# A deformable-convolution sampler regrouped by source rows, its TensorE part in a register-addressed loop

## What is computed

```
ys = base_y[None, None, :, None] + (ky * dil)[None, :, None, None] + dy
xs = base_x[None, None, None, :] + (kx * dil)[None, :, None, None] + dx
...
s = gather(img, y0b, x0b) * w00[None] + gather(img, y0b, x0b + 1) * w01[None] + gather(img, y0b + 1, x0b) * w10[None] + gather(img, y0b + 1, x0b + 1) * w11[None]
...
off1 = conv2d(x, w_off1, b_off1, stride=1, pad=1)
out = jax.nn.relu(bn_inf(deform_conv(x, off1, w_dc1, 1, 2, 2), g1, beta1, m1, v1))
off2 = conv2d(out, w_off2, b_off2, stride=1, pad=1)
out = bn_inf(deform_conv(out, off2, w_dc2, 1, 2, 2), g2, beta2, m2, v2)
out = out + x
return jax.nn.relu(out)
```

## Time and profile before

| | |
|---|---|
| three runs | 892.66, 894.47, 895.07 us; median 894.47 |
| profiled execution | 889.64 us, span 887.6 us |
| PE busy | 728.3 us (82%) |
| DVE, ACT, POOL busy | 484.3, 417.0, 161.4 us |
| mean granted TensorE clock | 0.86 |
| first sampler, from its first coordinates to the last ACT output | 40.1 to 257.4 us |
| second sampler, likewise | 286.1 to 507.0 us |
| attention and experts | 507 to 887.6 us |

### The profile page before, as it was taken

The page is one execution under the profiler, slowest core; times in us unless marked ns, Lnnn a source line. Parts: engine busy times, 40 slices in busy tenths (PEclk is TensorE's granted clock), DMA queues, the critical chain, the costliest instruction groups (busy, mean ns, idle before and its releaser), DMA issues.

```text
span 887.6 us, 40461 instructions
## 1 busy us (share of the span) xinstructions
PE 728.3 (82%) x18746; PEld 567.3 (64%) x18746; DVE 484.3 (55%) x840; ACT 417.0 (47%) x830; POOL 161.4 (18%) x190
## 2 busy tenths in 40 slices
PE   6787877788767887778788656999999999999546
PEld 2355555566633455555566545999999999998433
DVE  0565554455604645446455564666666666666654
ACT  1665455554315554546544143445445445545442
POOL 7000000000030000000000153343443443341300
PEclk8889878866769798887976578999999999999669
DMA  5400000000004000000000170000000000000002
GB/s 171 82 4 5 4 4 5 5 4 4 5 6 81 4 5 4 4 4 4 5 4 4 29 193 1 1 2 1 0 0 0 0 0 0 0 0 0 0 1 96
DMA packets 7835, 16.58 MB, mean 19 GB/s; under 512 B 1982, under 2 KB 5950, under 8 KB 7286
## 3 DMA queue, kind: packets, MB, share of 16 engines
q1 hardware_dynamic: 7678, 14.21, 6.3%
HBM read 10.34 MB, written 3.87 MB: 16 GB/s over the span
## 4 chain that ended last, share of the span: by engine, by line
PE 76%; issue 10%; DVE 6%; ACT 5%; POOL 1%; DMA 1%; SPq 0%; DVEq 0%
PE banks L227 20%; PE banks L145 14%; PE banks L696 7%; PE banks L680 7%; PE banks L726 6%; PE banks L458 4%; PE banks L737 4%; PE banks L716 3%; PE banks L691 2%; PE banks L180 2%; PE banks L166 2%; PE banks L707 2%; ACT hx L273 1%; DVE norm_stats L629 1%; ACT hy L278 1%
## 5 line engine op out<-in xcount | busy, mean ns | idle before, releaser
L227 PE MATMUL banks<-s,y 32*64 32x96 f32 (+9 forms) x10752 | 191.1, 268 | 66.0 <-issue 65.9
L318 DVE TENSOR_TENSOR s<-hy,hx 128x384 f32<-128x384 f32 (+3 forms) x336 | 144.4, 476 | 183.4 <-PE banks L227 181.8
L227 PEld LDWEIGHTS banks<-s,y 32*64 32x64 f32 x10752 | 160.2, 154 | 109.9 <-issue 100.2
L145 PE MATMUL banks<-w_dc,tiled 64*32 64x192 f32 x3584 | 130.2, 412 | 20.3 <-issue 13.7
L268 ACT COPY y<-banks 128x384 f32<-128x384 f32 x192 | 81.8, 484 | 114.0 <-PE banks L145 114.0
L145 PEld LDWEIGHTS banks<-w_dc,tiled 64*32 64x32 f32 x3584 | 74.3, 131 | 53.8 <-issue 26.6
L794 ACT COPY hy<-banks 128x512 f32<-128x512 f32 x64 | 37.6, 588 | 116.7 <-PE banks L726 116.7
L278 ACT ACTIVATE hy<-banks 128x512 f32<-128x512 f32 (+2 forms) x144 | 72.9, 583 | 38.4 <-PE banks L180 38.3
L898 POOL TENSOR_TENSOR y<-y,stats 128x1024 f32<-128x1024 f32 x33 | 62.8, 1902 | 142.2 <-DVE stats L839 142.2
L273 ACT ACTIVATE hx<-banks 128x384 f32<-128x384 f32 x144 | 61.4, 505 | 31.8 <-PE banks L166 23.9
L680 PE MATMUL banks<-src,s 128*128 (+1 forms) x560 | 75.0, 279 | 1.1 <-ACT src L617 1.1
(11 more groups left out here) (137 smaller groups left out, 876.9 us busy)
## 6 DMA issues: line engine op xcount, KB each, us to landing
src<-in_x_dram SPq DMA_DIRECT2D x4, 578.0 KB, 5.5
y<-in_w_dram SPq DMA_DIRECT2D x1, 2080.0 KB
off<-in_w_dram SPq DMA_DIRECT2D x2, 1024.0 KB
out_dram<-tokens SPq DMA_DIRECT2D x4, 512.0 KB, 2.6
offsets_dram<-tokens SPq DMA_DIRECT2D x32, 54.0 KB
off<-offsets_dram SPq DMA_DIRECT2D x16, 108.0 KB
w_dc<-in_w_dc_dram SPq DMA_DIRECT2D x2, 288.0 KB, 6.0
y<-in_w_attn_dram SPq DMA_DIRECT2D x1, 512.0 KB, 4.9
```

What stands on the lines that cost most here:

```text
L145: last = nc.tensor.matmul(m.ps[32 * j:32 * j + 32, FIRST_BANK + (count + g) % RING, (col % 2) * 192:(col % 2) * 192 + 192], m.tiled[rows, ...
L227: last = nc.tensor.matmul(out[:, r0:r0 + strip.n, first:first + width], m.y[32 * j:32 * j + 32, g, (s // 3) % 2 * Y_SLOTS + strip.slot, co ...
L318: nc.vector.tensor_tensor(dst, hy, hx[:, :, r0:r0 + strip.n, :], ALU.mult).then_inc(cv.s_ready, 1)
```

## The change

The sampler is regrouped. The outer loop now goes over the 8 source tile rows, the inner over the 9 taps: 72 steps per convolution, each with all 8 output rows of the window, inside the image or not.

- **PE** runs the 8 tile rows as a loop `with pe.Fori(0, TR) as i` with one body of nine taps; addresses in `off` and the values waited for come from registers.
- **Output.** A tile row adds into a 12-row band in PSUM (banks 0 to 3, 384 columns of each). After each tile row ACT copies the new rows to `tokens` in SBUF, DVE adds the band of the row before (L351), PE clears it.
- **x hats** are made for four new rows per step; the four others come from the block kept from the tile row before. So `s` is made by two products of 384 elements.
- **Slots.** An item (x, y or weighted) uses a pair of banks, two slots in turn; ACT takes a pair out with one instruction instead of two.
- **Weighted tiles** (`stage`, `yk`) are made for one tile row, three `ky` in six halves per row, placed behind the sampling of steps 0, 4, 5, 6, 7 and 8.
- **Coordinates** are built over all 128 partitions of `off` with a wider selection matrix (`near_sel`, 983 KB more to load), in six matmuls per step.
- **At the start** DVE clears `off` before the loads into it; the sampler waits for `moved[0]` and `moved[1]`; five weighted items instead of eight pairs come before it.
- The products and outputs of rows outside the image are not used.

```diff
+FIRST_COORDS = [("x", tap, -1) for tap in range(3)] + coords(0) + coords(1) + [("x", tap, -1) for tap in range(3, 6)]
+AHEAD = 2
+STEP_WEIGHTED = {0: (2, 1, 0), 4: (0, 0, 1), 5: (0, 1, 1), 6: (1, 0, 1), 7: (1, 1, 1), 8: (2, 0, 1)}
...
+def sampler_pe(nc, pe, m, cv):
+    old = 2 * cv.reach
+    for half in range(HALVES):
+        pe.wait_ge(cv.moved[half], MOVES)
...
+    with pe.Fori(0, TR) as i:
+        k = BEFORE_LOOP
+        for t in range(TAPS):
+            later, tap = divmod(t + AHEAD, TAPS)
+            pe.wait_ge(cv.emptied, i * PER_ROW + (k - 1))
+            columns_near(nc, m, cv, k, tap, new_rows(cv, tap) + TILE_ROWS * later, TILE_ROWS, i)
+            k += 1
+            pe.wait_ge(cv.emptied, i * PER_ROW + (k - 1))
+            rows_near(nc, m, cv, k, tap, first_row(cv, tap) + TILE_ROWS * later, i)
+            k += 1
+            if t == 0:
+                pe.wait_ge(cv.copied, i + COPIED_FROM)
+                pe.wait_ge(cv.added, i + (ADDED_FROM - 1))
+                pe.wait_ge(cv.cleared, 1)
+                for bank in range(PAIRS):
+                    nc.tensor.matmul(m.ps[:, bank, 0:OUT_ROWS * W], m.zeros[:, 0:P], m.zeros[:, 0:OUT_ROWS * W],
+                                     start=True, stop=True, skip_group_check=True)
+            if t in STEP_WEIGHTED:
+
+                pe.wait_ge(cv.emptied, i * PER_ROW + (k - 1))
...
+            pe.wait_ge(cv.s_ready, i * (2 * TAPS) + (2 * t + 2))
+            for col in range(TC):
...
+                                                s_rows(m, cv, t)[32 * j:32 * j + 32, :, g, at:at + width],
+                                                start=False, stop=True, skip_group_check=True)
+            last.then_inc(cv.sampled, 1)
+            if t in STEP_WEIGHTED:
+                weighted_near(nc, m, cv, k, *STEP_WEIGHTED[t][0:2])
+                k += 1
...
+def weighted_act(nc, act, m, cv, k, ky, part):
+    act.wait_ge(cv.filled, k + 1)
+    nc.scalar.copy(m.yk[:, ky, :, 2 * part:2 * part + 2, :].rearrange("p g a n -> p g (a n)"),
+                   slot_banks(m, k)[:, :, 0:384]).then_inc(cv.emptied, 1)
...
+    for tile_row in range(TR):
+        for t in range(TAPS):
+            if t == 2 and tile_row >= 2:
+                cv.rows_act(act, tile_row - 2)
+            for kind, *_ in step_items(tile_row, t):
+                if t == TAPS - 1 and kind == "w" and tile_row < TR - 1:
+                    act.wait_ge(cv.sampled, TAPS * (tile_row + 1))
...
+                    nc.scalar.copy(sum_rows(m, at, n), out_rows(m, first, n)).then_inc(cv.copied, 1)
+                item_act(nc, act, m, cv, k)
+                k += 1
...
+    for n in range(TR * TAPS):
+        if n + 1 < TR * TAPS:
+            hats(n + 1)
...
+        if n % TAPS == 0 and n // TAPS >= 2:
+            below = n // TAPS - 1
+            dve.wait_ge(cv.sampled, n)
+            dve.wait_ge(cv.copied, COPIED_FROM + below + 1)
...
+        weights(n)
```

More of the change, by code:

```diff
@@ L55, in near_strips @@
[L55 to L71, removed]
@@ L74, in near_columns @@
[L74 to L125, removed]
@@ new lines, in step_items @@
+def step_items(tile_row, tap):
+    items = coords(TAPS * tile_row + tap + AHEAD)
+    if tap in STEP_WEIGHTED:
+        ky, part, later = STEP_WEIGHTED[tap]
+        items.append(("w", ky, part, tile_row + later))
+    return items
+BEFORE_LOOP = len(FIRST_WEIGHTED) + len(FIRST_COORDS)
+PER_ROW = sum(len(step_items(0, tap)) for tap in range(TAPS))
+ITEMS = FIRST_WEIGHTED + FIRST_COORDS + [
+    item for tile_row in range(TR) for tap in range(TAPS) for item in step_items(tile_row, tap)]
+EMPTIED_AT = {item: k + 1 for k, item in enumerate(ITEMS)}
@@ new lines, with slot_banks, window, near_columns @@
+assert PER_ROW % 2 == 0
+def slot_banks(m, k):
+    return m.ps[:, FIRST_BANK + 2 * (k % 2):FIRST_BANK + 2 * (k % 2) + 2, :]
+def window(cv):
+    return TILE_ROWS + 2 * cv.reach, TILE_COLS + 2 * cv.reach, 2 - cv.reach
+def near_columns(cv, c, kx):
+    _, cols, ahead = window(cv)
+    at = TILE_COLS * c + ahead - 2 * kx
+    first = max(at, 0)
+    return first, min(at + cols, W) - first, first - at
+def weighted_near(nc, m, cv, k, ky, part):
+    for col in (2 * part, 2 * part + 1):
+        for j in range(4):
+            for g in range(2):
+                image = IMAGES[g][j]
+                rows = slice(C * (image % 2), C * (image % 2) + C)
+                last = nc.tensor.matmul(
+                    m.ps[32 * j:32 * j + 32, FIRST_BANK + 2 * (k % 2) + g, (col % 2) * 192:(col % 2) * 192 + 192],
+                    m.stage[rows, image // 2, col, :], cv.w_dc[rows, 3 * ky:3 * ky + 3, :],
+                    start=True, stop=True, skip_group_check=True)
+    last.then_inc(cv.filled, 1)
@@ new lines, in columns_all @@
+def columns_all(nc, pe, m, cv, count, h, tap, col):
+    pe.wait_ge(cv.all_emptied, count - RING + 2)
+    for g in range(2):
+        rows = group_rows(g, 1)
+        nc.tensor.matmul(m.ps[:, FIRST_BANK + (count + g) % RING, :],
+                         m.sel[rows, (TILE_COLS * col - 2 * (tap % 3) + 4) // 2, :],
+                         m.off[rows, tap, HALF_ROWS * W * h:HALF_ROWS * W * (h + 1)],
+                         start=True, stop=True, skip_group_check=True).then_inc(cv.all_filled, 1)
```

579 lines of the change are left out of this document (345 added, 234 removed).

## The result

The changed kernel takes 968.18 us (median of 4 runs, 967.68 to 971.83) against 894.77 us: a ratio of 1.0818 with a 95% interval of 1.076 to 1.0876, slower by 73 us. Forecast were 927 us and a range of 873 to 965. All times are medians of a kernel's runs on one chip beside new runs of the kernel before; two kernels, e1_pad2 and e7_pad50, have one run each in a slower state of the chip, and their other runs alone have medians of 923.5 and 923.9 us.

A forecast was written before the change was run, and what follows sets the result against it. PE was taken to be bound by its instruction supply, 128 matmuls per 3.73 us. Profiled 889.6 us, plus 33 for 16 tile rows of 28.0 us and their ends, plus 4.8 to the median, gave 927 us, range 873 to 965.

The forecast's parts named there:

- the loop stays: Likeliest case, both samplers: PE's loop isn't fetched anew, steps paced by the two-slot chain; +4 to +57 us, chance 0.48.
- rival 3: PE's loop body doesn't stay, one packet's 3.73 us per back edge: +42 us on top of +33, 948 to 969 us, chance 0.20.
- a two-slot chain: Sampler steps: PE in order with two slots, next sampling waits behind ACT's emptying of the weighted item; 25.7 us per row.
- Weighted step: Six of nine sampler steps: sampling, weighted products, ACT's copy, hand-overs and y coordinates in series, 3.06 us at clock 1.00.
- The other steps: Three sampler steps without weighted products: coordinates, ACT, hat and products, 4.0 us spread over two steps, 2.0 us each.
- The row boundary: End of a tile row: ACT's copy and DVE's sum before PE may clear, about 1.3 us left over, bounds 0.4 and 2.4.
- The clock: PE's mean granted clock in the samplers taken as 0.85, 70% of the time at 1.00, against 0.80 before.
- R = 28.0: Sampler time per tile row at the mixed clock, 28.0 us; with change = 16R − 415.1 it gives +33 us.
- Rival 2: Faster, the samplers' chain is short enough: R below 25.9 us, such as clock 1.00 throughout; 871 to 891 us, chance 0.26.
- Beginnings: Samplers wait for both halves of the offsets and so start later: +1.7 us in the first, +2.9 us in the second.
- Costed at nothing: Clearing of `off`, larger tables (+7 us if not hidden), stage copies, address instructions (+52 us if on the path), wider coordinate matmuls.
- The rule: Against the change: loop body of 6.7 packets, 31% more than any loop shown to stay, just fills or passes 8 blocks.

The follow-up runs named there:

- e1_pad2: Changed kernel with 30 tiny matmuls of zeros ahead of the second sampler's coordinates: 928.07 us, ratio 1.0307 to the kernel before.
- e7_pad50: Changed kernel with 50 tiny matmuls of zeros ahead of the second sampler's coordinates: 926.04 us, ratio 1.0242 to the kernel before.
- e9_again: Changed kernel once more, unaltered, on the same chip as the padded ones: 972.39 us, ratio 1.0857 to the kernel before.
- e11_pad30: Second run of the changed kernel with 30 tiny matmuls of zeros ahead of the second sampler's coordinates: 923.41 us, ratio 1.030 to the kernel before.
- e3_short: Changed kernel with only 6 tiny matmuls of zeros ahead of the second sampler's coordinates: 992.08 us, ratio 1.0999 to the kernel before.

## Why the prediction was wrong, point by point

**What bounds the kernel before: right.** One packet of 128 matmuls per 3.73 us. The written-out kernels draw 6 or 7 packets per row as computed.

**The step that failed: "the loop stays", taken for both convolutions from the body's length.** The prediction counted 6.7 packets for the body, saw that with the partly used blocks at both ends they just fill or pass 8 blocks, and gave the loss 0.20 without asking where each copy starts. The runs show that this place decides: the same 1,717 instructions touch 7 blocks and stay in the first convolution, and touch 8 and are lost in the second. The forecast had no wait for instructions; the second sampler has 37.6 us of it in seven rows, and one copy lost costs 44 to 47 us (second sampler 277.4 us in e9_again and 280.8 in the changed kernel against 233.6 in e11_pad30).

**The price in rival 3: half of it.** It took one packet's 3.73 us at each back edge, 26 us less what the boundary hides, "+21 us for one convolution". Seven rows of the changed kernel take 43.4 us more than those of e11_pad30 (241.08 against 197.64). Waiting for instructions adds 36.3 us (37.6 against 1.3), for a first and a second block in each pass; matmuls at the lower granted clock add 18.3 us (PE busy 165.82 against 147.55 us, clock 0.84 against 0.96); and 11 us less is spent on waits for ACT and DVE (37.3 against 48.4). That the supply of the rest is "hidden under the 28" held: the packets, 9 per pass (8 blocks and one ahead, not 6.7), bring hardly any further wait. That the time, 968, lies among those of rival 3 (948 to 969) is luck: that sum had both convolutions lost at a low price, in truth it is one at twice the price.

**The forecast itself, a loop that stays and a two-slot chain: right where the loop stays.** With the second loop placed, two kernels in three measurements take 928.07, 923.41 (the same kernel twice) and 923.26 us; 927 were forecast. That it is this near is in part luck, since the terms miss in both directions:
- Weighted step 3.06 us: measured 3.28. ACT's copy of 768 at 0.80 us and sampling at 0.92 us were right; the hand-overs were too short, 0.16 us and not 0.09 until ACT starts, 0.14 and not 0.05 back, and 0.38 and not 0.32 for the y coordinates.
- The other steps 2.0 us: measured 2.25, 1.58 and 2.25 us, mean 2.03. PE from 57 to 64 us:

```profile
57.17 0.99 PE L214 MATMUL banks<-s,y 32*64 32x80 f32 x64
...
59.42 1.00 PE L214 MATMUL banks<-s,y 32*64 32x64 f32 x64 [0.68 <-DVE s L327]
...
61.00 1.00 PE L214 MATMUL banks<-s,y 32*64 32x96 f32 x64
...
63.25 1.02 PE L214 MATMUL banks<-s,y 32*64 32x80 f32 x61 [0.63 <-DVE s L327]
```

- The row boundary 1.3 us: 26.43 − 6×3.28 − 6.08 leaves 0.7 us; more of it is hidden.
- Row at clock 1.00: 25.7 forecast, 26.43 measured in the first sampler, 27.60 in the second, where DVE's four added operations go with 1.2 us more per row, 9.6 us over eight (4.8 us were allowed for them).
- The clock: 0.85 forecast, 0.99 measured in the first sampler, 0.84 in the second (seven rows of each by stretch, below). The loops that stay get 0.93 to 1.00 (0.93 in the first sampler of e9_again). So R = 28.0 came out nearly right (26.66 and 28.23 in e11_pad30) from a chain 0.7 to 1.9 us too short and a clock too low. Rival 2, all at 1.00, had the clock right for the first sampler, but its R of 25.9 isn't reached there either.
- Beginnings: coordinates at 44.7 us, not 42, held by the offsets' transfer (9.82 us of idle time, released by it). Its last DMA is issued 1.6 us later than before (37.89 against 36.30 us). The first sampler starts 4.6 us later than before and the second 4.0, where 1.7 and 2.9 were forecast.

The seven rows of each sampler of the changed kernel, for the clock:

```profile
51.65:238.16 186.51, 142.45 (x5784) 97.61 (x5783) 113.65 (x259) 109.04 (x181) 7.35 (x28) 0.99 0.00 1
305.83:546.91 241.08, 165.82 (x5784) 109.76 (x5783) 122.53 (x284) 109.01 (x181) 7.35 (x28) 0.84 0.02 4
```

**Costed at nothing:** address instructions, rightly (a resident row is its chain of waits, and written out, without them, it is no shorter). For the larger tables and the clearing no run says whether they have a part in the 2.7 us by which the first coordinates came later than forecast.

**The rule.** The prediction's estimate from the size that the Trainium skill states was a warning that it weighed too low. The Trainium skill, "Runtime: NRT & Kernel Launch", section on instruction fetch mechanics, states 128 KiB for PE in blocks of 16 KiB, refilled as a FIFO: by estimate, 8 blocks. By that rule, the runs agree: 7 touched blocks and one ahead stay, and with more than a few instructions in an 8th they don't. Its other sentence, that a branch out of a window of two pages forces a fetch, disagrees: 7 blocks back, the branch takes 0.21 us, and the measurement decides.

**Open:** why a lost loop is lost at every back edge or only at some; the 5.2 us behind the samplers (the granted clock was 0.71 there in the first 52 us and 0.80 in the first 45 before, which would go with it, but nothing was tried); and what sets the clock.

## What to carry to other kernels

A hardware loop on PE needs a body that stays (lost in one convolution the kernel takes 968 us, written out 930), and that goes by the blocks it touches, not by its length: count the instructions, look for the border in the pauses of straight code, and check each copy of the loop on its own by packets per pass and by idle time at the back edge. If one is lost, some cheap instructions in a place where PE waits anyway can bring it back (some 44 us here). And where supply was the limit, taking it away shows the next chain at once: here it was two slots and a product standing behind the sampling, and only with that reordered as well did the change beat the kernel before (882.6 against 897.7 us in the same set).

## What the runs showed of the hardware

- A lost loop isn't lost evenly: with about 3, 13, 23 and 159 of its instructions in the 8th block, 0, 2, 3 and 7 of 7 back edges waited, 4.6 to 5.1 us each for 13 and 23, 4.0 to 4.7 us for 159.
- A back edge of a loop that stays takes 0.21 to 0.26 us, over 1,717 instructions.
- In a lost pass the waits stand at its beginning: 36.2 of 37.6 us in seven passes at the back edge and just behind it, though packets come all through the pass.
- The loops that lost every back edge had lower granted clocks, 0.84 and 0.85 (changed kernel and e3_short, e9_again); loops that stayed had 0.93 to 1.00, the one written out 0.94 to 0.99. The same first sampler had 1.00 in one execution (e11_pad30) and 0.93 in another (e9_again), with 8 us between them. In the changed kernel a stretch at 0.50, of 7 to 14 us, began within 3 to 6 us of the start of each of the seven lost back edges' branches: a strip's sampling took 1.50 us at 374.22 us and 0.99 at 383.37.
